# Two transposes taken off TensorE and the weights' means put on GpSimd, in a fused attention and FFN block

## The reference

```
q, k, v = split(layernorm(x) @ w_qkv) per head        # S=2048 rows, D=128, H=16 heads of 8
w       = relu(q @ k.T / sqrt(8))                     # per head, 2048 x 2048
attn    = (w / (sum(w) + 1e-6)) @ v
y       = layernorm(x) + attn @ w_out + b_out
x1      = x + (layernorm(y) * gamma + beta)
z       = layernorm(x1)
x2      = x1 + sqrt((z @ cos(theta + theta_noise))**2 + (z @ sin(phi + phi_noise))**2)
```

## Time and profile before

| What | Value |
|---|---|
| Median of 3 runs | 408.98 us (408.88 to 409.05) |
| Profiled execution | 409.39 us, of it 407.6 us span |
| TensorE busy | 400.2 us, 98% |
| ScalarE busy | 335.8 us, 82% |
| VectorE busy | 327.3 us, 80% |
| GpSimd busy | 57.3 us, 14% |
| Granted TensorE clock, mean | 0.999 |

### The profile page before, as it was taken

The page is one execution under the profiler, slowest core; times in us unless marked ns, Lnnn a source line. Parts: engine busy times, 40 slices in busy tenths (PEclk is TensorE's granted clock), DMA queues, the critical chain, the costliest instruction groups (busy, mean ns, idle before and its releaser), DMA issues.

```text
span 407.6 us, 9110 instructions
## 1 busy us (share of the span) xinstructions
PE 400.2 (98%) x3579; PEld 103.9 (25%) x3579; DVE 327.3 (80%) x648; ACT 335.8 (82%) x595; POOL 57.3 (14%) x70
## 2 busy tenths in 40 slices
PE   8999999999999999999999999999999999999995
PEld 5332222222222222222222322222222222222233
DVE  5867888898888888777888888777778888777856
ACT  4868888987888898888888888889888898889863
POOL 1461000089201010002201010000100001000111
PEclk9999999999999999999999999999999999999999
DMA  6128831010030101001021101001012000000200
GB/s 173 41 53 157 170 101 53 2 51 2 9 90 29 53 2 51 4 14 47 21 80 31 53 2 26 27 2 54 26 54 58 1 27 2 27 0 28 71 1 27
DMA packets 11742, 17.56 MB, mean 43 GB/s; under 512 B 3684, under 2 KB 5364, under 8 KB 11316
## 3 DMA queue, kind: packets, MB, share of 16 engines
q1 hardware_dynamic: 11556, 16.84, 15.5%
q10 hardware_dynamic: 144, 0.13, 0.2%
HBM read 3.99 MB, written 5.11 MB: 22 GB/s over the span
## 4 chain that ended last, share of the span: by engine, by line
PE 95%; DVE 3%; DMA 1%; ACT 0%; issue 0%; SPq 0%; DVEq 0%
PE pv L1194 61%; PE sc L1160 28%; PE pv L1060 5%; DMA wqkv_sb<-w_qkv_dram 1%; PE pv L1201 0%; DVE x L1006 0%; PE sc L1306 0%; DVE x L1024 0%; DVE stats_p L894 0%; ACT w_buf L642 0%; DVE mag L1016 0%; PE sc L1118 0%; DVE stats L759 0%; PE sc L1201 0%; DVE q_rep L786 0%
## 5 line engine op out<-in xcount | busy, mean ns | idle before, releaser
L1194 PE MATMUL pv<-w_buf,v_sb 128*9 128x512 f32 x2048 | 267.4, 594 | 0.0
L813 DVE TENSOR_SCALAR w_buf<-sc 128x512 f32<-128x512 f32 x256 | 177.0, 691 | 65.3 <-PE sc L1160 52.9
L634 ACT ACTIVATE w_buf<-sc 128x512 f32<-128x512 f32 x256 | 153.2, 598 | 56.6 <-PE sc L1160 56.5
L642 ACT ACTIVATE w_buf<-sc 128x512 f32<-128x512 f32 (+1 forms) x254 | 182.9, 720 | 0.0
L1160 PE MATMUL sc<-q_rep,k_rep 32*128 32x512 f32 x1024 | 130.7, 496 | 0.1
L820 DVE TENSOR_SCALAR w_buf<-sc 128x512 f32<-128x512 f32 (+1 forms) x181 | 124.2, 686 | 0.0
L1160 PEld LDWEIGHTS sc<-q_rep,k_rep 32*128 32x128 f32 x1024 | 49.6, 181 | 218.4 <-ACT w_buf L634 183.5
L1194 PEld LDWEIGHTS pv<-w_buf,v_sb 128*9 128x9 f32 x2048 | 32.7, 89 | 64.1 <-ACT w_buf L642 36.4
L522 POOL TENSOR_TENSOR oT<-o_raw,o_scale 128x512 f32<-128x512 f32 (+1 forms) x4 | 5.1, 1284 | 85.2 <-issue 61.8
L528 POOL TENSOR_TENSOR x<-x,mv 128x512 f32<-128x512 f32 (+1 forms) x5 | 4.4, 871 | 71.5 <-DVE x L921 59.7
L538 POOL TENSOR_TENSOR mag<-sq 128x256 f32<-128x256 f32 x6 | 4.4, 732 | 67.7 <-ACT sq L681 67.7
(11 more groups left out here) (135 smaller groups left out, 140.1 us busy)
## 6 DMA issues: line engine op xcount, KB each, us to landing
pv_dram<-pv_sb SPq DMA_DIRECT2D x15, 256.0 KB, 2.0
q_rep<-q_hi SPq DMA_DIRECT2D x30, 64.0 KB, 2.1
q_rep<-q_lo SPq DMA_DIRECT2D x30, 64.0 KB, 2.1
k_rep<-k_hi SPq DMA_DIRECT2D x6, 256.0 KB, 4.2
k_rep<-k_lo SPq DMA_DIRECT2D x6, 256.0 KB, 5.5
x_sb<-x_dram SPq DMA_DIRECT2D x3, 256.0 KB, 4.5
o_raw<-pv_dram SPq DMA_DIRECT2D x3, 256.0 KB
o_scale<-inverse_dram SPq DMA_DIRECT2D x3, 256.0 KB
```

The source lines that it names most:

```text
L634: nc.scalar.activation(w_buf[:, s % W_STEPS, 0, :], early[:, 0, :], ACT.Relu).then_inc(relu[0], 2 if none else 1)
L642: nc.scalar.activation(w_buf[:, s % W_STEPS, 2:2 + n, :], late[:, 0:n, :], ACT.Relu).then_inc(relu[0], 1)
L813: nc.vector.tensor_scalar(w_buf[:, s % W_STEPS, 1, :], early[:, 1, :], 0.0, None, ALU.max).then_inc(relu[1], 2 if both else 1)
L1194: last = nc.tensor.matmul(bank[32 * i:32 * i + HD + 1, :], v_sb[:, k, HPG * g + i, 0:HD + 1], w_buf[:, s % W_STEPS, i, :], start=(k == 0), ...
```

## The change

- **x1** of passes 0 to 2 is no longer transposed by TensorE. VectorE transposes blocks of 32 by 32 (`blocks_of_x1`, at (1, 10)), SP writes the result to DRAM and fetches it back in four DMAs that put the blocks in their places (`place_blocks`). The copy by ScalarE is gone.
- **The last chunk of x** takes the same way: VectorE's blocks at (0, 1) of the first pass, then SP. Its keys are projected at (0, 6), behind those of chunks 2 and 0 and the first queries, and they are split last. Other projections move one place forward.
- **FFN weights' means**: VectorE transposes blocks, sums along them and transposes again at (3, 13) (`partial_sums`), SP sends the four partial sums through DRAM and spreads them to all partitions (`w_sums`), GpSimd adds them, scales and subtracts (`centre_ffn_w`). `eps_std` is turned by VectorE at (2, 0).
- Statistics of chunks 1 to 3 move, statistics of x1 come in two pieces, and the relu tables change.

The core of the diff:

```diff
-FIRST_BOTH_LATE = ((4, 11, 13, 15), (3, 10, 12, 14), (3, 5, 6, 10, 12), (5, 13))
-DVE_BOTH_LATE = ((), (), (8,), (11,))
-BOTH_LATE = ((3, 7, 11, 14, 15), (3, 5, 6, 8, 9, 11, 15), (3, 7, 11, 15), (3, 7, 11, 15))
+FIRST_BOTH_LATE = ((11, 13, 15), (3, 10, 12, 14), (3, 5, 6, 10, 12), (5, 10, 13))
+DVE_BOTH_LATE = ((), (), (8,), (8,))
+BOTH_LATE = ((3, 7, 11, 14, 15), (3, 5, 6, 8, 9, 10, 12, 13, 15), (3, 7, 11, 15), (3, 7, 11, 15))
...
+                def place_blocks(src, n, dst, ready, turn, saved, done):
+
+                    sp.wait_ge(ready, turn)
+                    sp.dma_start(blocks_dram[n], src).then_inc(saved, 16)
+                    sp.wait_ge(saved, 16 * turn)
+                    blocks = blocks_dram[n].rearrange("(q a) (t b c) -> b a t q c", q=4, b=4, c=32)
+                    for b in range(4):
+                        sp.dma_start(dst[32 * b:32 * b + 32, :].rearrange("a (t q c) -> a t q c", q=4, c=32),
+                                     blocks[b]).then_inc(done, 16)
...
+                    if c == 1:
+                        place_blocks(x1[:, :, :].rearrange("p t d -> p (t d)"), 1, xT[:, 3 * CW:4 * CW],
+                                     x3_blocks, 1, x3_saved, x3_loaded)
...
+                        if c == 1 and g == 0:
+                            sp.wait_ge(w_part_ready, 1)
+                            for q in range(4):
+                                sp.dma_start(sums_dram[q], w_turned[32 * q:32 * q + 2 * D // 32, :]).then_inc(w_part_saved, 16)
+                            sp.wait_ge(w_part_saved, 64)
+                            sp.dma_start(w_sums[:, :, :].rearrange("p q n -> p (q n)"),
+                                         sums_dram.rearrange("q m i -> (q m i)").partition_broadcast(P)
+                                         ).then_inc(w_sums_loaded, 16)
                         if c < NC - 1:
                             next_queries(c, g)
                         save_values(c, g)
+                        if g == 0 and c > 0:
+                            place_blocks(y[:, :, :].rearrange("p t d -> p (t d)"), 0, x1T[:, :],
+                                         x1_blocks, c, x1_saved, x1T_loaded)
...
+                def centre_ffn_w():
+
+                    both = ffn_w[:, :, :].rearrange("p c d -> p (c d)")
+                    pool.wait_ge(w_sums_loaded, 16)
+                    for n, (a, b) in enumerate(((0, 1), (2, 3), (0, 2))):
+                        if n == 2:
+                            pool.wait_ge(w_sums_own, 2)
+                        nc.gpsimd.tensor_tensor(w_sums[:, a, :], w_sums[:, a, :], w_sums[:, b, :],
+                                                ALU.add).then_inc(w_sums_own, 1)
+                    pool.wait_ge(w_sums_own, 3)
+                    nc.gpsimd.tensor_scalar(w_sums[:, 0, :], w_sums[:, 0, :], 1 / D, None,
+                                            ALU.mult).then_inc(w_sums_own, 1)
+                    pool.wait_ge(w_sums_own, 4)
+                    nc.gpsimd.tensor_tensor(both, both, w_sums[:, 0, :], ALU.subtract).then_inc(ffn_w_ready, 1)
...
                 nc.gpsimd.memset(eps_col[:, :], LN_EPS).then_inc(eps_ready, 1)
+                centre_ffn_w()
                 scale_o(0, G)
                 finish(Part(0))
...
+                def blocks_of_x1(part):
+
+                    nc.vector.transpose(y[:, :, :].rearrange("p t d -> p (t d)"),
+                                        x1[:, :, :].rearrange("p t d -> p (t d)")).then_inc(x1_blocks, 1)
...
                     return [((0, 13), lambda: project_out(part)),
-                            ((1, 11), lambda: transpose_x1(part)), ((2, 4), lambda: ffn(part, 0)),
+                            ((2, 4), lambda: ffn(part, 0)),
...
                 run_pass(0, [((0, 0), lambda: transpose_x(2)), ((0, 1), lambda: project_v(1)),
-                             ((0, 2), lambda: project_k(2)), ((0, 3), lambda: transpose_x(3)),
-                             ((0, 4), lambda: project_k(3)), ((0, 5), lambda: project_k(0)),
-                             ((0, 6), lambda: project_q(0)), ((0, 7), lambda: project_v(2)),
-                             ((0, 9), lambda: project_v(3))]
-                         + [((c, 7), lambda c=c: project_q(c)) for c in range(1, NC)] + [((3, 11), ffn_means)])
+                             ((0, 2), lambda: project_k(2)), ((0, 3), lambda: project_k(0)),
+                             ((0, 4), lambda: project_q(0)), ((0, 5), lambda: project_v(2)),
+                             ((0, 6), lambda: project_k(3)), ((0, 8), lambda: project_v(3))]
+                         + [((c, 7), lambda c=c: project_q(c)) for c in range(1, NC)])
```

More of the change, by code:

```diff
@@ L147, in block_kernel @@
         var_eps = sb("var_eps", [P, NT])
-        eps_std = sb("eps_std", [P, NT])
-        eps_T = sb("eps_T", [NT, P])
+        eps_std = sb("eps_std", [P, 32])
+        eps_turned = sb("eps_turned", [P, 32])
+        w_blocks = sb("w_blocks", [P, 2 * D])
+        w_part = sb("w_part", [P, 32])
+        w_turned = sb("w_turned", [P, 32])
+        w_sums = sb("w_sums", [P, 4, 2 * D])
+        sums_dram = nc.dram_tensor("sums_dram", [4, 2 * D // 32, 32], F32).ap()
         eps_spread = sb("eps_spread", [P, NC, H * CW // P])
@@ L247, in block_kernel @@
         x1T_done = sem("x1T_done")
+        x1_blocks = sem("x1_blocks")
+        x3_blocks = sem("x3_blocks")
+        x3_saved = sem("x3_saved")
+        x3_loaded = sem("x3_loaded")
+        x1_saved = sem("x1_saved")
+        x1T_loaded = sem("x1T_loaded")
         x1T_ready = sem("x1T_ready")
@@ L606, in take_v @@
                 def take_v(c):
-                    root(c)
+                    if c != 1:
+                        root(c)
                     act.wait_ge(v_done, c + 1)
@@ L674, in take_x1T @@
                 def take_x1T(part):
-                    act.wait_ge(x1T_done, part.n + 1)
+                    act.wait_ge(x1T_done, part.half + 1)
                     nc.scalar.copy(x1T[:, part.cols()], part.x1_bank[:, 0:part.tiles * P]).then_inc(x1T_ready, 1)
@@ L884, in residual @@
                         dve.wait_ge(xb_ready, 2 * NC - 1)
+                    if part.j > 0:
+                        dve.wait_ge(x1_saved, 16 * part.j)
                     dve.wait_ge(proj_done, part.n + 1)
@@ L895, in post_stats, with x1_stats @@
                     part.chain(last)
+                def x1_stats(part, piece):
+                    for t in part.all()[2 * piece:2 * piece + 2]:
+                        last = nc.vector.bn_stats(stats_p[:, t, :], x1[:, t, :])
+                    if piece == 1:
+                        part.chain(last)
                 def post_inverse(part, norm):
-                    nc.vector.memset(spare[:, :], 0.0)
+                    if norm == 1:
+                        nc.vector.memset(spare[:, :], 0.0)
                     for t in part.all():
@@ L1225, in transpose_x1 @@
                     pe.wait_ge(x1_ready, part.n + 1)
-                    if part.half is None:
-                        pe.wait_ge(pv_out, G * part.j + G + 1)
                     transpose_tiles(part.x1_bank, lambda t: x1[:, t, :], part.all(), x1T_done)
[L1230 to L1238, removed]
-                                        ident[:, :]).then_inc(means_done, 1)
                 def ffn(part, i):
                     n, tiles, bank = part.pieces()[i]
+                    if part.j == 0 and i == 0:
+                        pe.wait_ge(ffn_w_ready, 1)
                     if i == 0:
-                        pe.wait_ge(x1T_ready, part.n + 1)
+                        if part.half is None:
+                            pe.wait_ge(x1T_loaded, 64 * (part.j + 1))
+                        else:
+                            pe.wait_ge(x1T_ready, part.half + 1)
                         if part.half is None:
```

104 lines of the change are left out of this document (64 added, 40 removed).

## The result

The changed kernel takes 416.46 us (median of 4 runs, 415.27 to 416.78) against 409.01 us. The ratio is 1.0176, with a 95% interval of 1.0155 to 1.0197: slower by 7.5 us. The profiled execution took 416.35 us, with a span of 414.5 us, 6.9 us more than before. Of all executions of the kernels in this text one, of the kernel with x1's part alone, took 545.0 us at a mean granted clock of 0.66, and the ratios leave it out.

What follows compares the result with a forecast made beforehand. It took TensorE, busy 400.2 of 407.6 us, as the bound. Terms +0.5 - 0.77 - 1.76 + 6.8 + 1.6 = +6.4 us on the 408.98 us median gave 415.4 us, range 411.0 to 419.5 (chance 0.82).

Steps and rivals of the forecast that it cites:

- Removed work: TensorE loses x1's transposes in three passes (-1.76 us), the means (-0.77) and first-pass work (-0.73): -3.26 us together.
- Wait one: First pass, step 16: TensorE waits 1.25 us for group 1's late keys, starting 0.5 us later than before.
- The last chunk's keys: First pass, step 7: the last chunk's loads land near 22 us, before TensorE wants them at 24.7; cost 0.
- Wait two: Second pass, first output projection: TensorE waits for GpSimd's product, held behind w_sums; +6.8 us, 4.2 to 9.4.
- The clock: After the stall at the second pass's first projection, TensorE runs at 1.2 GHz for 3.2 us: +1.6 us, 0 to 3.4.
- R1: First pass, steps 7 and 8: slow 128-byte pieces make TensorE wait for xT; +3 us, 418.4 us; chance 0.15.
- R2: Second pass, first projection: stall only 3.6 us and no clock lost; +1.6, 410.6 us; chance 0.12.
- R3: Second pass, first projection: w_sums early, GpSimd late by little, kernel not slower; -2.0, 407.0 us; chance 0.06.

Runs made afterwards that it cites:

- old first pass: Changed kernel with GpSimd's oT product ahead of centring the FFN weights, and x's last chunk again transposed by TensorE in the earlier order: 407.01 us, ratio 0.9946.
- product first: Changed kernel with GpSimd's product for the first output projection put ahead of centring the FFN weights: 407.51 us, ratio 0.9958.
- sums first: Changed kernel, GpSimd's order kept, with SP's DMAs for the FFN weights' sums issued ahead of the last group's first-pass save: 407.69 us, ratio 0.9961.

## Why the prediction was right, step by step

It forecast 415.4 us (profiled 415.8, +6.4) and 416.46 was measured (profiled 416.35, +7.0). The direction, the place and the order of size came from one question put to SP's and GpSimd's orders: what is queued behind the instruction that now waits, and who waits for that.

- **Removed work**: forecast -0.77 and -1.76, measured -0.63 (with 0.14 lost in step 63) and -2.03 (a step at 242.25 that took 0.29 us too long before is a plain one after). Step 63 is a plain one with x1's part alone and takes 1.56 us in the old first pass, so the 0.14 come with the means' part or the relu table of that group; that VectorE's partial sums, which stand there, are the cause is argued, not tested. x1's part alone gave -1.6 by the medians and -2.0 by its trace. In the first pass, from the first scores to those of step 15, 0.83 us are gone where 0.73 were forecast.
- **Wait one**: forecast 1.25 us at step 16, measured 1.41; start of step 16 at +0.5 forecast, +0.70 measured, of it 0.12 from before the first scores. GpSimd's last split, SP's extra copies and the landing followed as worked out: group 1's first issue came at 29.72, where 28.31 + 1.35 = 29.66 was forecast.
- **The last chunk's keys** were costed at 0, and TensorE did not wait for them. But the slack was smaller than I worked out. The store to DRAM took 4.2 us to land, not 2.5:

```profile
14.63 0.59 SPq L401 DMA_DIRECT2D blocks_dram<-x  x1
18.86 2.72 SPq L405 DMA_DIRECT2D xT<-blocks_dram  x4
```

The last of the four loads, under way at 21.0 to 21.3 us, landed 3.1 us from its issue at 20.9, so at 24.0 against TensorE's 24.64: 0.6 us of slack where I had 2.7. In the DMA view of that stretch:

```profile
xT<-blocks_dram SPq DMA_DIRECT2D x1, 64.0 KB, 3.1
```

- **Wait two**: forecast 6.8 us, measured 6.52. Here errors cancelled, so that it came so close is luck. `w_sums` was issued at 128.75, 1.0 us later than worked out, as the inverses' way took longer (`o_scale` 0.7 us later than before) and the four sums landed slower. Its landing took 3.6 us instead of my 5.0, 1.4 less: twice the bytes of `o_scale` for about the same time. The scaling on GpSimd took 0.85 us instead of 0.45, above even the 0.73 that I gave as its most. The fit of the Trainium skill, page "DMA: Bandwidth & Descriptors", section "Anatomy of one DMA", which is for another issuing engine, gave an estimate of 3.2 us. The trace has 3.6, so here the page was nearer than my term.
- **The clock**: forecast 1.6 us, measured 2.4; this is the mis-sized term. That it would fall was right. I took about the 3 us of the warm-up for the time until it is back, and here 5.1 us of work passed. The row doesn't show that time: it is the length of the twelve matmuls. In the kernel before full rate happens to follow them; in the changed kernel the next four matmuls still took 1.09 us instead of 0.63.
- **Rivals.** R1, slow pieces: false, though the loads landed 2 us later than worked out. While the loads ran, 321 packets, all under 512 bytes, took 63.7% of 16 engines over 0.4 us (20.3 to 20.7), that is 4.1 us or 13 ns each:

```profile
DMA packets 321, 0.04 MB, mean 102 GB/s; under 512 B 321, under 2 KB 321, under 8 KB 321
...
q1 hardware_dynamic: 321, 0.04, 63.7%
```

The Trainium skill's warning on the page "VectorE: DVE Perf Modes", section "The three transpose paths", does not touch a transpose whose 32 by 32 blocks VectorE turns first, so that each DMA run is 128 bytes long. R2 and R3 are false as to the stall; product first and sums first show what R3 would have been worth, 407.5 and 407.7, where I wrote 407.0.

## What to carry to other kernels

An engine with 15% of busy time is still a queue: before putting independent work on it, list what stands behind the new wait and when that is wanted, and put the work behind it, not ahead. A stall of TensorE can cost more than its length: here 6.5 us of waiting cost 8.9, as TensorE came back at half clock. And a part that saves 0.7 us can lose it again in a copy that waits for all pieces at once; waiting for the last piece where it is used kept the gain.

## What the runs showed of the hardware

- **The clock.** TensorE's last work before the stall ended at 137.59 - 6.52 = 131.07, and the clock fell at 135.9, after 4.8 us of idleness. At the end of the kernel before it fell after 3.4 us. At the end of the changed kernel TensorE's last work ended at 410.19, and the 2.50 us from 412.00 have a mean of 0.57, so it fell at about 412.35, after 2.2. Behind the stall it rose after 5.1 us of work. At the start of the kernel before the matmuls have their full rate from 4.45 us on; in the changed kernel two that start at 5.11 still took 1.33 us instead of 0.88. So neither time can be taken from one row.
- **A store to DRAM of 256 KB** landed in 4.2 us in the first pass; x1's three, of the same size, landed in 2.0, 3.4 and 2.0 us. In the last two of the 4.2 us, from 17 to 19, the DMA engines were busy 3% of the time at most, so it wasn't spent moving data. The cause is open.
- **VectorE's block transpose** of 128x512 took 0.70 us, about as long as the operation of that size in the earlier trace rows (0.69).
- **VectorE beside GpSimd.** In the first pass of the changed kernel two VectorE additions of 128x4, 0.17 us long elsewhere, took 1.04 and 0.58 us. Each ended within 0.03 us of a GpSimd instruction, at 22.80 beside 22.78 and 27.06 beside 27.03:

```profile
21.76 1.04 DVE L831 TENSOR_SCALAR var_eps<-mv 128x4 f32<-128x4 f32 x1
...
26.48 0.58 DVE L831 TENSOR_SCALAR var_eps<-mv 128x4 f32<-128x4 f32 x1
```

```profile
21.51 1.27 POOL L522 TENSOR_TENSOR k_lo<-raw,k_hi 128x512 fp32r<-128x512 f32 x1
...
26.42 0.61 POOL L520 CAST k_hi<-raw 128x512 fp32r<-128x512 f32 x1 [1.73 <-ACT raw L663]
```

In the kernel before one took 0.41 us and ended at 19.32 beside the end of a GpSimd instruction at 19.30. It looks as if this VectorE instruction waited for GpSimd's to end. No run tested it.
